# Attention block: the second key tile's mask taken out of the score matmuls and put behind the exponentials, three heads on GpSimd, one on VectorE

## The chip, the cores and the metric

One core of a Trainium2 chip runs the whole program. The metric is the device time in microseconds (us) of one execution. The engines work side by side, each through its own list of instructions in order: TensorE (PE) multiplies matrices into PSUM, ScalarE (ACT) does exponentials and copies, VectorE (DVE) and GpSimd (POOL) do elementwise work, SyncE (SP) issues the transfers.

## The reference, cut to what matters

A decoder block for 8 batches of 512 tokens with 256 features: a two-direction Mamba block, then attention with 16 heads, then a feed-forward block whose neurons spike over 5 steps. The parts around the change:

```python
scores = jnp.einsum('bhqd,bhkd->bhqk', q, k) / math.sqrt(D_HEAD)      # D_HEAD = 16
scores = jnp.where(mask == 0, jnp.float32(-1000000000.0), scores)
attn = jax.nn.softmax(scores, axis=-1)
out = jnp.einsum('bhqk,bhkd->bhqd', attn, v)
...
h = jnp.square(jax.nn.relu(jnp.einsum('bsd,fd->bsf', x, W_fc)))
y = jnp.einsum('bsf,df->bsd', h, W_proj)
def step(mem, _):                                   # 5 times, spikes are counted
    reset = spike_fn(mem - THRESHOLD)
    mem_new = BETA * mem + y - reset * THRESHOLD
    return (mem_new, spike_fn(mem_new - THRESHOLD))
```

## The kernel before, in words

The program has two passes. `mamba_pass` takes the first 1,600 us and isn't touched. `attention_pass` then loops over the 8 batches (`b`), about 135.6 us each. There is no scheduler: every engine's order is the order of the code, and semaphores (`wait_ge`, `then_inc`) tie them together.

A batch begins with 16 heads of prescores, of which DVE takes row maxima (L1897); between them PE does feed-forward work of the next batch. Then comes the **attention stage**, on which all of this document turns. It has 8 **units** (0 to 7); a unit is four heads (`hh` 0 to 3) and two key tiles of 128 keys (`t` 0 and 1), and it is done in two **halves** of two heads. PE's order in it is: `score(unit + 1, half)`, `weigh(unit, half)`, for both halves of all units, with a transpose (`to_tokens`, L1513) after the second `weigh` of units 2, 4 and 6.

- `score` (L1473) writes the two key tiles of a head into one of two PSUM pairs. A tile costs one matmul for the scores (`pair<-q_st,k_st`), and where it is masked there, a second that adds the mask (`pair<-mask_biasT,ident_bf`). A head waits until ACT has read the head before the last from its pair (`s_exp`).
- ACT (L1692) turns a pair into exponentials in `pr`, one instruction of 1024 columns a head.
- GpSimd (`mask_exp`, L2017, its instruction on L2024) multiplies the second tile of heads 1 and 3 by words that are 0 or 1. So those tiles have no mask matmul: `ON_POOL = ((1,), (3,))`, one head a half, from unit 1 on.
- `weigh` (L1490) multiplies `pr` by the values. Its first half takes the first key tile and waits for the unit's last exponential; its second half takes the second tile and waits for GpSimd's second mask of the unit (`s_kept`).

Meanwhile DVE counts the spikes of the batch before, on 128x1024 tiles: `start` (L1815), and four `step`s of three instructions each (L1825, L1827, L1829; step 1 has L1821 and L1823 instead of the first two), `finish` (L1834), which makes the output tile `tmp` that SP stores. Between them stand `norm_apply` (L1746), which writes `xn_q` for the next batch, and `normalise(g)` (L1799 and L1803), which waits for the transpose of unit 2g+2 (the last for the one after unit 7). GpSimd's part of the norm is `rstd_of` (L1972, L1974), ahead of its masks. After the stage, ACT's `project_k` (L1653) writes `qk`, which lies over `mem`, `cnt` and `tmp`; it waits for the store (`s_out`). The last batch has no next one, so no `norm_apply` and no `project_k`.

Of the kernel before, what the change touches and what calls it, by code (L numbers as in the profile page):

```python
# [14 lines left out]
H, DH = 16, 16  # L15
P = 128
# [6 lines left out]
QR = 6 * DH + 3  # L23
EPS = 1e-5
MASKED = -float(2 ** 32)
FLOOR = -3.0e38
STEPS, BETA, THRESHOLD = 5, 0.9, 1.0
# [13 lines left out]
_cols()  # L41


ON_POOL = ((1,), (3,))
Q_PART = [0, 0, 1, 0, 2, 1]
K_PART = [0, 1, 0, 2, 0, 1]

# [1118 lines left out]
def attention_pass(nc, ctx, a, mid, out, sb, where, stage, psum, consts, handover, early, late):  # L1166

    f32, bf16, i32 = mybir.dt.float32, mybir.dt.bfloat16, mybir.dt.int32
    ALU, ACT, AX = mybir.AluOpType, mybir.ActivationFunctionType, mybir.AxisListType
    ident, cols, minus_half, col, settle, s_const = consts  # L1170
    pair, bank, y_bank, general = psum
# [6 lines left out]
    pr = sb("pr", [P, 4, TT, T], f32, where["g1"])  # L1178
# [5 lines left out]
    y_sb = sb("y_sb", [P, TT, D])  # L1184
# [6 lines left out]
    mask_biasT = sb("mask_biasT", [P, TT, T], bf16)  # L1191
# [5 lines left out]
    q_st = sb("q_st", [P, H, T], bf16)  # L1197
    k_st = sb("k_st", [P, H, T], bf16)
# [12 lines left out]
    mem, cnt, tmp = (sb(name, [P, TT, D], f32, where["qk"] + 4 * KB * n)  # L1211
                     for n, name in enumerate(("mem", "cnt", "tmp")))
# [48 lines left out]
    m_cut = stage("m_cut", ahead=1)  # L1261
    s_sc = stage("score")
    s_exp = stage("exp", ahead=2)
    s_kept = stage("masked_exp")
    s_word = stage("mask_words")
    g_out = stage("g_out")
    out_ready = stage("out_ready")
# [1 line left out]
    with nc.Block() as block:  # L1269
# [102 lines left out]
        def _(pe):  # L1372
            pe.wait_ge(handover.sem, handover.count(0))

            def mm(o, lhsT, rhs, start=True, stop=True):
                return pe.matmul(o, lhsT, rhs, start=start, stop=stop)  # L1376
# [96 lines left out]
            def score(b, unit, half):  # L1473

                g, s = unit // 2, unit % 2
                if unit == H // 4 and half == 0:
                    pe.wait_ge(s_mr[1].sem, s_mr[1].count(b))
                for hh in (2 * half, 2 * half + 1):
                    hd = 4 * g + hh
                    n = b * 2 * H + unit * 4 + hh  # L1480
                    pe.wait_ge(s_exp.sem, s_exp.count(n - 2))
                    for t in range(2):
                        kt = 2 * s + t
                        on_pool = unit > 0 and t == 1 and hh in ON_POOL[half]
                        last = mm(pair[hh % 2][:, t, :], k_st[0:QR, hd, kt * P:(kt + 1) * P], q_st[0:QR, hd, :], True, on_pool)
                        if not on_pool:
                            last = mm(pair[hh % 2][:, t, :], ident_bf[:, :], mask_biasT[:, kt, :], False, True)
                    last.then_inc(s_sc.sem, 1)

            def weigh(b, unit, half, it):  # L1490

                g, s = unit // 2, unit % 2
                if half == 0 or unit == 0:
                    pe.wait_ge(s_exp.sem, s_exp.count(b * 2 * H + unit * 4 + 3))
                else:
                    pe.wait_ge(s_kept.sem, s_kept.count(b * (H - 2) + unit * 2 - 1))
                key = ("av", g)
                if s == 0 and half == 0:
                    pe.wait_ge(*G.free(key, it))
                bk = G.bank(key, it)  # L1500
                kt = 2 * s + half
                for hh in range(4):
                    last = mm(bk[32 * hh:32 * hh + 32, :], v_sb[:, kt, 4 * g + hh, :], pr[:, hh, kt, :],
                              kt == 0, kt == TT - 1)
                if kt == TT - 1:
                    last.then_inc(G.full_sem(key), 1)
# [45 lines left out]
            for k in range(TT):  # L1552
                last = mm(bank[0], ones_bf[:, :], keep_bf[:, k, :], k == 0, k == TT - 1)
# [167 lines left out]
        def _(dve):  # L1721
# [71 lines left out]
            def normalise(g, it):  # L1793

                dve.drain()
                dve.wait_ge(*G.full(("ot", g), it))
                bk = G.bank(("ot", g), it)
                o = bk[:, :].rearrange("p (j h e) -> p j h e", j=TT, h=4)
                dve.reciprocal(rsum[:, :, :], o[:, :, :, DH:DH + 1].squeeze(3))  # L1799
                dve.drain()  # L1800
                dst = o_sb[:, :, g * 4 * DH:(g + 1) * 4 * DH].rearrange("p j (h e) -> p j h e", h=4)
                for j in range(TT):
                    last = dve.tensor_tensor(dst[:, j], o[:, j, :, 0:DH],  # L1803
                                             rsum[:, j, :].unsqueeze(2).broadcast_to((P, 4, DH)), ALU.mult)
                last.then_inc(G.done_sem(("ot", g)), 1)

            def spikes(beta, cols_of=(A3,)):


                def start():  # L1810
                    dve.wait_ge(s_out.sem, s_out.count(beta - 1))
                    settle(dve)
                    dve.drain()
                    for c in cols_of:
                        dve.tensor_scalar(cnt[c], y_sb[c], THRESHOLD, None, ALU.is_gt)  # L1815

                def step(i):
                    for c in cols_of:
                        dve.drain()
                        if i == 1:  # L1820
                            dve.scalar_tensor_tensor(tmp[c], y_sb[c], BETA, y_sb[c], ALU.mult, ALU.add)  # L1821
                            dve.drain()
                            dve.scalar_tensor_tensor(mem[c], y_sb[c], THRESHOLD, tmp[c], ALU.is_gt, ALU.subtract)  # L1823
                        else:
                            dve.scalar_tensor_tensor(tmp[c], mem[c], -BETA, y_sb[c], ALU.mult, ALU.add)  # L1825
                            dve.drain()
                            dve.scalar_tensor_tensor(mem[c], mem[c], -THRESHOLD, tmp[c], ALU.is_lt, ALU.subtract)  # L1827
                        dve.drain()
                        dve.scalar_tensor_tensor(cnt[c], mem[c], -THRESHOLD, cnt[c], ALU.is_lt, ALU.add)  # L1829

                def finish():
                    dve.drain()
                    for c in cols_of:
                        dve.scalar_tensor_tensor(tmp[c], cnt[c], 1.0 / STEPS, x_res[c], ALU.mult, ALU.add).then_inc(out_ready.sem, 1)  # L1834
                return start, step, finish
# [52 lines left out]
            dve.memset(y_sb[A3], 0.0)  # L1888
            dve.memset(x_res[A3], 0.0)

            def batch(b, it, more):
                for hd in range(H):
                    for j in range(TT):
                        dve.wait_ge(s_max.sem, s_max.count((b * H + hd) * TT + j - 2))
                        dve.wait_ge(s_pre.sem, s_pre.count((b * H + hd) * TT + j))
                        settle(dve)
                        dve.tensor_tensor_reduce(  # L1897
                            masked[:, j % 2, :], bank[j], mask_bias[:, j, :], 1.0, FLOOR, ALU.add, ALU.max, m_col[:, j, hd:hd + 1]).then_inc(s_max.sem, 1)
                start, step, finish = spikes(b)
                if more:  # L1900
                    add_down(b + 1, it)
                    norm_stats(ATT, x1n)
                start()
                step(1)
                if more:
                    norm_apply(ATT, b + 1, x1n, xn_q)
                step(2)
                if isinstance(it, int):
                    dve.wait_ge(early.mid.sem, early.mid.count(B))
                normalise(0, it)  # L1910
                step(3)
                normalise(1, it)
                step(4)
                finish()
                normalise(2, it)
                normalise(3, it)
                if more:
                    cut_lo(b + 1, 0)

                dve.wait_ge(x1_set.sem, x1_set.count(b))  # L1920
                for jj in range(TT // 2):
                    dve.wait_ge(*G.full(("wo", jj), it))
                    bk = G.bank(("wo", jj), it)
                    dve.tensor_tensor(two(x_res, jj), two(x1, jj), bank_tiles(bk), ALU.add).then_inc(G.done_sem(("wo", jj)), 1)
                    dve.drain()
                    for j in (2 * jj, 2 * jj + 1):
                        dve.bn_stats(stats[:, j, :], x_res[:, j, :])
                norm_mean(FF2)
                if more:
                    cut_last(b + 1, 0)  # L1930
                    take_v(0, it)
                norm_apply(FF2, b, x_res, xn)
                if more:
                    take_q(it)
                    cut_lo(b + 1, 1)
                    take_v(1, it)
                    cut_last(b + 1, 1)
                    dve.wait_ge(*G.done(("fn", KD - 1), it))
                    first_norm(b + 2)
# [239 lines left out]
```

## Time and profile before

| what | value |
|---|---|
| median of 3 runs | 2750.9 us (2750.63 to 2751.59) |
| the profiled execution: its own time | 2753.34 us |
| its span, first to last instruction | 2751.6 us |
| mean granted TensorE clock | 0.982 |
| PE busy | 2629.1 us, 96% |
| DVE busy | 2192.3 us, 80% |
| ACT busy | 1742.5 us, 63% |
| POOL busy | 1719.2 us, 62% |

Busy shares are means over both passes. Rows of the timeline give start and duration in us; where one row holds several instructions (x4), its duration is from the first start to the last end. A time in brackets is how long the engine sat idle before the row, and for what. In the text "us 1982" means 1982 us after the span's start; batch 2 is the one that is read, and its attention stage runs from us 1967 to us 2012.

### The profile page before, as it was taken

How to read it: one execution, taken by the hardware profiler on the slowest of the kernel's cores; microseconds unless marked ns; L12 is line 12 of the kernel's file. 1: busy time of each engine (PE TensorE's matmuls, PEld its weight loads, DVE VectorE, ACT ScalarE, POOL GpSimd, SP SyncE). 2: the span in 40 equal slices, each digit the busy share in tenths (PEclk: the TensorE clock that was granted, in tenths of full speed). 3: DMA queues.
4: the chain of work that ended last, by engine and by line, in shares of the span. 5: the costliest groups of instructions: out<-in, count | busy, mean ns of one | idle time of the engine just before them, and what ended most of it. 6: DMA issues, size and time to landing. Idle time of an engine off the chain costs nothing. (4 is left out here: it accounts for less than half of the span.)

```text
span 2751.6 us, 55526 instructions
## 1 busy us (share of the span) xinstructions
PE 2629.1 (96%) x19177; PEld 1799.8 (65%) x19210; DVE 2192.3 (80%) x3270; ACT 1742.5 (63%) x2871; POOL 1719.2 (62%) x966
## 2 busy tenths in 40 slices
PE   6999999999999999999999879999999999999996
PEld 3887787787878877877887754545454545454523
DVE  5999999999999999999998949494848485858573
ACT  4878877877987788788778433545454444444342
POOL 3889989988988889899899813332323232323130
PEclk9999999999999999999999999999999999999978
DMA  3122212212221221222123051404040404040300
GB/s 123 43 79 73 85 44 81 89 43 79 74 80 43 80 82 58 70 67 95 37 78 102 9 182 55 123 2 122 2 122 2 122 2 122 2 122 2 107 2 16
DMA packets 102089, 187.07 MB, mean 68 GB/s; under 512 B 14720, under 2 KB 75264, under 8 KB 100256
## 3 DMA queue, kind: packets, MB, share of 16 engines
q1 hardware_dynamic: 101840, 183.92, 21.4%
q8 instruction: 135, 2.21, 0.3%
q14 instruction: 114, 0.93, 0.1%
HBM read 148.38 MB, written 35.52 MB: 67 GB/s over the span
## 5 line engine op out<-in xcount | busy, mean ns | idle before, releaser
L981 DVE TENSOR_TENSOR_SCAN h<-dA,pair 128x512 f32<-128x512 f32 x1024 | 1171.2, 1202 | 113.6 <-PE pair L475 102.9
L1120 POOL TENSOR_TENSOR hC<-h,C_rep 128x1024 f32<-128x1024 f32 x512 | 1201.4, 2368 | 93.5 <-DVE h L981 87.3
L718 ACT ACTIVATE dA<-delta,cols 128x511 f32<-128x511 f32 x1024 | 664.2, 711 | 41.7 <-DVE h L981 25.6
L475 PE MATMUL pair<-diagB,duT 64*128 64x128 f32 x8192 | 549.3, 281 | 23.1 <-DVE h L981 14.1
L475 PEld LDWEIGHTS pair<-diagB,duT 64*128 64x128 f32 x8192 | 485.9, 188 | 125.7 <-issue 90.1
L575 PE MATMUL y_bank<-ident,hC 128*128 128x128 f32 x4112 | 539.4, 278 | 5.0 <-POOL hC L1120 4.1
L575 PEld LDWEIGHTS y_bank<-ident,hC 128*128 128x128 f32 x4112 | 458.3, 141 | 96.9 <-issue 55.1
L1897 DVE CUSTOM_DVE_ANT_0 masked<-pair,mask_bias 128x512 f32<-128x512 f32 x512 | 321.8, 688 | 19.4 <-PE pair L1376 13.5
L1629 ACT ACTIVATE pr<-pair 128x1024 f32<-128x1024 f32 x256 | 248.3, 1021 | 74.3 <-PE pair L1376 74.3
L2001 POOL CAST m_part<-m_rest 8x512 bf16<-8x512 f32 x16 | 9.6, 603 | 414.4 <-ACT m_rest L1629 414.4
L475 PE MATMUL general<-xnT,w_in 128*128 128x512 f32 x496 | 241.9, 602 | 4.5 <-ACT xnT L718 3.5
L2024 POOL TENSOR_TENSOR pr<-pr,keep_word 128x512 int32<-128x512 int32 x112 | 162.7, 1455 | 117.6 <-ACT pr L1629 115.4
L1376 PE MATMUL general<-w_down,g 128*128 128x256 f32 x1024 | 232.5, 380 | 1.3 <-DVEq L1724 1.3
L1376 PEld LDWEIGHTS general<-w_down,g 128*128 128x128 f32 x1024 | 193.7, 190 | 33.8 <-issue 5.9
L1376 PE MATMUL pair<-q_st,k_st 99*128 99x512 bf16 x512 | 196.2, 383 | 5.5 <-ACT pr L1629 3.5
L1376 PE MATMUL general<-xT,w_up 128*128 128x512 f32 x360 | 168.2, 604 | 1.2 <-ACT xT L1629 0.7
L1376 PE MATMUL pair<-k_st,q_st 96*128 96x512 bf16 x512 | 151.6, 404 | 6.9 <-DMA q_st<-qk_parts 4.2
L991 DVE SCALAR_TENSOR_TENSOR u<-general,cols,u 128x511 f32<-128x511 f32 (+2 forms) x192 | 142.0, 740 | 13.3 <-ACT u L718 9.4
L1376 PE MATMUL pair<-mask_biasT,ident_bf 128*128 128x512 bf16 x368 | 140.3, 381 | 0.0
L1376 PEld LDWEIGHTS pair<-q_st,k_st 99*128 99x128 bf16 x512 | 50.1, 98 | 135.9 <-ACT pr L1629 91.0
L1972 POOL TENSOR_SCALAR rstd<-mv 128x4 f32<-128x4 f32 x24 | 15.6, 650 | 196.3 <-DVE mv L1739 193.7
L1376 PEld LDWEIGHTS pair<-k_st,q_st 96*128 96x128 bf16 x512 | 50.2, 98 | 113.2 <-DVE m_col L1897 83.5
(185 smaller groups left out, 3197.1 us busy)
## 6 DMA issues: line engine op xcount, KB each, us to landing
C_rep<-c_rows SPq DMA_DIRECT2D x128, 512.0 KB, 4.2
qk_parts<-qk_part SPq DMA_DIRECT2D x96, 256.0 KB, 4.2
w_in<-w_in SPq DMA_DIRECT2D x16, 1024.0 KB, 4.9
k_st<-qk_parts SPq DMA_DIRECT2D x8, 1536.0 KB, 9.1
q_st<-qk_parts SPq DMA_DIRECT2D x8, 1536.0 KB, 9.4
x_in<-x SPq DMA_DIRECT2D x18, 512.0 KB, 5.3
w_out<-w_out SPq DMA_DIRECT2D x17, 512.0 KB, 4.2
mid<-x_out SPq DMA_DIRECT2D x9, 512.0 KB, 4.8
```

The source lines that it names most:

```text
L475: return pe.matmul(o, lhsT, rhs, start=start, stop=stop)
L575: last = pe.matmul(y_bank[:, c * P:(c + 1) * P], hC[:, g % RING, i, c * P:(c + 1) * P], ident[:, :], start=j == 0 and i == 0 and c == 0, s ...
L718: return act.activation(o, i, fn, **kw)
L981: last = dve.tensor_tensor_scan(h[:, g % 4, i, :], dA[:, g % 4, i, :], dBu[:, i, :], 0.0, ALU.mult, ALU.add)
L991: dve.scalar_tensor_tensor(u[n][:, k, lag:T], raw[:, 0:T - lag], col("fb"[n] + "conv_w", CW * k + CW - 1 - lag), u[n][:, k, lag:T], ALU.mu ...
L1120: pool.tensor_tensor(hC[:, g % RING], h[:, g % 4], C_rep[:, 2 * j:2 * j + 2, :], ALU.mult).then_inc(s_hC.sem, 1)
L1376: return pe.matmul(o, lhsT, rhs, start=start, stop=stop)
L1629: return act.activation(o, i, fn, **kw)
L1897: dve.tensor_tensor_reduce(masked[:, j % 2, :], bank[j], mask_bias[:, j, :], 1.0, FLOOR, ALU.add, ALU.max, m_col[:, j, hd:hd + 1]).then_in ...
L1972: pool.tensor_scalar(rstd[:, :], mv[:, :, 1], EPS, None, ALU.add)
L2001: pool.tensor_copy(high, m_rest[:, :])
L2024: pool.tensor_tensor(words, words, keep_word[:, unit % 2, :].unsqueeze(1).broadcast_to((P, len(heads), T)), ALU.mult).then_inc(s_kept.sem, 1)
```

## The change

The second key tile of all four heads, from unit 1 on, is masked behind its exponential. GpSimd takes heads 0 and 1 in the first half (one instruction of two heads) and head 3 in the second. DVE takes head 2: a new `keep_exp(b, unit)` waits for that head's exponential and takes the minimum of it and mask plus 2^32 (2^32 where a key is kept, 0 where not). Its calls stand among the passes that count spikes; `step` now takes `parts`, so that calls can stand inside a step, and `finish` moves behind `normalise(2)` and `keep_exp(b, 7)`. `weigh` of a second half waits for both engines.

```diff
-ON_POOL = ((1,), (3,))
+ON_POOL = ((0, 1), (3,))
+ON_DVE = ((), (2,))
...
-                        on_pool = unit > 0 and t == 1 and hh in ON_POOL[half]
-                        last = mm(pair[hh % 2][:, t, :], k_st[0:QR, hd, kt * P:(kt + 1) * P], q_st[0:QR, hd, :], True, on_pool)
-                        if not on_pool:
+                        kept_later = unit > 0 and t == 1 and hh in ON_POOL[half] + ON_DVE[half]
+                        last = mm(pair[hh % 2][:, t, :], k_st[0:QR, hd, kt * P:(kt + 1) * P], q_st[0:QR, hd, :], True, kept_later)
+                        if not kept_later:
                             last = mm(pair[hh % 2][:, t, :], ident_bf[:, :], mask_biasT[:, kt, :], False, True)
...
                 else:
+                    pe.wait_ge(s_kept_dve.sem, s_kept_dve.count(b * (H // 2 - 1) + unit - 1))
                     pe.wait_ge(s_kept.sem, s_kept.count(b * (H - 2) + unit * 2 - 1))
...
+            def keep_exp(b, unit):
+
+                for half in range(2):
+                    for hh in ON_DVE[half]:
+                        dve.wait_ge(s_exp.sem, s_exp.count(b * 2 * H + unit * 4 + hh))
+                        exps = pr[:, hh, 2 * (unit % 2) + 1, :]
+                        dve.scalar_tensor_tensor(exps, mask_biasT[:, 2 * (unit % 2) + 1, :], -MASKED, exps,
+                                                 ALU.add, ALU.min).then_inc(s_kept_dve.sem, 1)
...
                 step(1)
+                keep_exp(b, 1)
                 if more:
                     norm_apply(ATT, b + 1, x1n, xn_q)
-                step(2)
+                step(2, (0, 1))
+                keep_exp(b, 2)
+                step(2, (2,))
+                step(3, (0,))
                 if isinstance(it, int):
                     dve.wait_ge(early.mid.sem, early.mid.count(B))
+                keep_exp(b, 3)
                 normalise(0, it)
-                step(3)
+                step(3, (1,))
+                keep_exp(b, 4)
+                step(3, (2,))
                 normalise(1, it)
-                step(4)
+                keep_exp(b, 5)
+                step(4, (0, 1))
+                keep_exp(b, 6)
+                step(4, (2,))
+                normalise(2, it)
+                keep_exp(b, 7)
                 finish()
-                normalise(2, it)
                 normalise(3, it)
```

DVE's order from the end of step 1, before (`pr` are the exponentials, `mem`, `cnt` and `tmp` the spikes' state, count and scratch; L1799 and L1803 are `normalise(0)`):

```order
L1829 SCALAR_TENSOR_TENSOR cnt<-mem,cnt 128x1024
L1746 TENSOR_SCALAR xn_q<-x1n,mv_7223,rstd_7224 128x256 [waits ln1_rstd]
L1746 TENSOR_SCALAR xn_q<-x1n,mv_7223,rstd_7224 128x256 x3
L1825 SCALAR_TENSOR_TENSOR tmp<-mem,y_sb 128x1024
L1827 SCALAR_TENSOR_TENSOR mem<-mem,tmp 128x1024
L1829 SCALAR_TENSOR_TENSOR cnt<-mem,cnt 128x1024
L1799 RECIPROCAL rsum<-general 128x16 [waits mid_dma,ot_full]
L1803 TENSOR_TENSOR x_out<-general,rsum 128x64 x4
```

The same place now (lines behind the new functions are 2 to 27 further down; L1904 is `keep_exp`):

```order
L1836 SCALAR_TENSOR_TENSOR cnt<-mem,cnt 128x1024
L1904 SCALAR_TENSOR_TENSOR pr<-mask_biasT,pr 128x512 [waits exp]
L1749 TENSOR_SCALAR xn_q<-x1n,mv_7223,rstd_7224 128x256 [waits ln1_rstd]
L1749 TENSOR_SCALAR xn_q<-x1n,mv_7223,rstd_7224 128x256 x3
L1827 SCALAR_TENSOR_TENSOR tmp<-mem,y_sb 128x1024
L1833 SCALAR_TENSOR_TENSOR mem<-mem,tmp 128x1024
L1904 SCALAR_TENSOR_TENSOR pr<-mask_biasT,pr 128x512 [waits exp]
L1836 SCALAR_TENSOR_TENSOR cnt<-mem,cnt 128x1024
L1827 SCALAR_TENSOR_TENSOR tmp<-mem,y_sb 128x1024
L1904 SCALAR_TENSOR_TENSOR pr<-mask_biasT,pr 128x512 [waits exp,mid_dma]
L1802 RECIPROCAL rsum<-general 128x16 [waits ot_full]
L1806 TENSOR_TENSOR x_out<-general,rsum 128x64 x4
```

The `keep_exp` of unit 1 now stands ahead of `xn_q`, and that of unit 2 behind `xn_q` and two of step 2's passes.

At the end of the stage DVE now has (the last pass of step 4, `normalise(2)`, unit 7, `finish`):

```order
L1836 SCALAR_TENSOR_TENSOR cnt<-mem,cnt 128x1024
L1802 RECIPROCAL rsum<-general 128x16 [waits ot_full]
L1806 TENSOR_TENSOR x_out<-general,rsum 128x64 x4
L1904 SCALAR_TENSOR_TENSOR pr<-mask_biasT,pr 128x512 [waits exp]
L1841 SCALAR_TENSOR_TENSOR tmp<-cnt,x_res 128x1024
```

Unit 7's instruction stands behind `normalise(2)`, which waits for the transpose after unit 6 (`ot_full`).

PE's second half of a unit, before (`score` of heads 2 and 3, then `weigh`):

```order
L1376 MATMUL pair<-q_st,k_st 128x512 [waits exp]
L1376 MATMUL pair<-mask_biasT,ident_bf 128x512
L1376 MATMUL pair<-q_st,k_st 128x512
L1376 MATMUL pair<-mask_biasT,ident_bf 128x512
L1481 REGISTER_ALU
L1376 MATMUL pair<-q_st,k_st 128x512 [waits exp]
L1376 MATMUL pair<-mask_biasT,ident_bf 128x512
L1376 MATMUL pair<-q_st,k_st 128x512
L1496 REGISTER_ALU
L1376 MATMUL general<-pr,v_sb 32x512 [waits masked_exp]
L1376 MATMUL general<-pr,v_sb 32x512 x3
```

And now:

```order
L1378 MATMUL pair<-q_st,k_st 128x512 [waits exp]
L1378 MATMUL pair<-mask_biasT,ident_bf 128x512
L1378 MATMUL pair<-q_st,k_st 128x512
L1483 REGISTER_ALU
L1378 MATMUL pair<-q_st,k_st 128x512 [waits exp]
L1378 MATMUL pair<-mask_biasT,ident_bf 128x512
L1378 MATMUL pair<-q_st,k_st 128x512
L1498 ISA
L1499 ISA [waits masked_exp_dve]
L1378 MATMUL general<-pr,v_sb 32x512 [waits masked_exp_pool]
L1378 MATMUL general<-pr,v_sb 32x512 x3
```

One mask matmul of the half is gone (six matmuls in `score` instead of seven; the first half likewise), and `weigh` has a second wait.

## Rows read from the trace of the kernel before

**Rows 1.** The page: busy times; the chain that ended last, by engine.

```profile
PE 2629.1 (96%) x19177; PEld 1799.8 (65%) x19210; DVE 2192.3 (80%) x3270; ACT 1742.5 (63%) x2871; POOL 1719.2 (62%) x966
...
PE 33%; DVE 3%; issue 2%; ACT 1%; POOLq 1%; DMA 1%; POOL 0%; DVEq 0%; ACTq 0%
```

**Rows 2.** The chain in order of time, us 1960 to 2100: start, duration, what.

```profile
1979.51 1.63 PE pair L1376 x7
...
2009.88 1.28 POOL pr L2024
2011.20 1.06 PE y_bank L1376 x8
```

**Rows 3.** Timeline of PE: start, duration, engine, line, operation, names, shapes.

```profile
1979.44 0.39 PE L1376 MATMUL pair<-q_st,k_st 99*128 99x512 bf16 x1
1979.67 0.38 PE L1376 MATMUL pair<-mask_biasT,ident_bf 128*128 128x512 bf16 x1
...
1982.07 0.39 PE L1376 MATMUL pair<-q_st,k_st 99*128 99x512 bf16 x1
...
1986.33 1.06 PE L1376 MATMUL y_bank<-pr,v_sb 128*32 128x512 f32 x8
```

**Rows 4.** Timeline of ACT: exponentials of units 1 and 2, then unit 3.

```profile
1975.27 1.94 ACT L1629 ACTIVATE pr<-pair 128x1024 f32<-128x1024 f32 x2 [0.73 <-PE pair L1376]
...
1982.35 0.60 ACT L1629 ACTIVATE xT<-general 128x512 f32<-128x512 f32 x1
1983.15 1.94 ACT L1629 ACTIVATE pr<-pair 128x1024 f32<-128x1024 f32 x2 [0.20 <-PE pair L1376]
```

**Rows 5.** Timeline of DVE: step 2 of the spikes, in batch 2.

```profile
1979.93 1.23 DVE L1825 SCALAR_TENSOR_TENSOR tmp<-mem,y_sb 128x1024 f32<-128x1024 f32 x1
1981.23 2.15 DVE L1827 SCALAR_TENSOR_TENSOR mem<-mem,tmp 128x1024 f32<-128x1024 f32 x1
1983.46 2.15 DVE L1829 SCALAR_TENSOR_TENSOR cnt<-mem,cnt 128x1024 f32<-128x1024 f32 x1
```

**Rows 6.** Timeline of POOL: the norm's `rstd`, then masks.

```profile
1974.54 1.96 POOL L1974 TENSOR_TENSOR rstd<-rstd,minus_half 128x4 f32<-128x4 f32 x1
...
1980.01 2.29 POOL L2024 TENSOR_TENSOR pr<-pr,keep_word 128x512 int32<-128x512 int32 x1 [0.64 <-ACT pr L1629]
1982.64 1.89 POOL L2024 TENSOR_TENSOR pr<-pr,keep_word 128x512 int32<-128x512 int32 x1 [0.34 <-ACT pr L1629]
```

**Rows 7.** Queries by line: durations in ns, min/median/max, first and last start.

```profile
L2024 POOL TENSOR_TENSOR pr<-pr,keep_word x112: 1262/1292/2302, 1705.7 to 2685.0; 128x512 int32<-128x512 int32 x112
...
L1984 POOL TENSOR_TENSOR x1n<-x_in,x_mid x8: 2350/2358/2365, 1607.8 to 2447.6; 128x1024 f32<-128x1024 f32 x8
...
L1746 DVE TENSOR_SCALAR xn_q<-x1n,mv,rstd x32: 401/414/1373, 1621.0 to 2521.7; 128x256 f32<-128x256 f32 x32
```

**Rows 8.** Timeline of DVE: a 512-column pass in the tail, GpSimd idle.

```profile
2731.09 0.69 DVE L1827 SCALAR_TENSOR_TENSOR mem<-mem,tmp 128x512 f32<-128x512 f32 x1
```

**Rows 9.** Timeline of DVE at the end of batch 2's stage: `normalise(2)`.

```profile
2009.99 0.26 DVE L1799 RECIPROCAL rsum<-general 128x16 f32<-128x16 f32 x1 [3.00 <-PE general L1513]
2010.33 0.62 DVE L1803 TENSOR_TENSOR x_out<-general,rsum 128x64 f32<-128x64 f32 x4
```

**Rows 10.** Timeline of PE: an idle stretch of the last batch.

```profile
2700.43 1.12 PE L1384 MATMUL general<-ident,xn 128*128 128x128 f32 x4 [5.10 <-DVE xn L1746]
```

**Rows 11.** Windows of 1 us there: length, PE, PEld, DVE, ACT, POOL busy, PEclk.

```profile
2698.00:2699.00 1.00, 0.00 (x0) 0.00 (x0) 0.01 (x1) 0.00 (x0) 0.96 (x1) 0.67 0.00 0
...
2707.00:2708.00 1.00, 1.00 (x2) 0.34 (x1) 0.00 (x0) 0.97 (x2) 0.00 (x0) 0.50 0.00 0
...
2709.00:2710.00 1.00, 1.00 (x4) 0.47 (x3) 0.00 (x0) 0.41 (x1) 0.00 (x0) 1.00 0.00 0
```

**Rows 12.** After the stage: ACT's `project_k`; the transfers' time to landing (median us).

```profile
2014.22 0.69 ACT L1629 ACTIVATE qk<-general,cols 128x512 f32<-128x512 f32 x1 [1.29 <-PE general L1376]
...
out<-tmp SPq DMA_DIRECT2D x8, 512.0 KB, 2.9
```

More of the change, by code:

```diff
@@ L1263, in attention_pass @@
     s_exp = stage("exp", ahead=2)
-    s_kept = stage("masked_exp")
+    s_kept = stage("masked_exp_pool")
+    s_kept_dve = stage("masked_exp_dve")
     s_word = stage("mask_words")
@@ L1815, in start, with step @@
                         dve.tensor_scalar(cnt[c], y_sb[c], THRESHOLD, None, ALU.is_gt)
-                def step(i):
+                def step(i, parts=(0, 1, 2)):
                     for c in cols_of:
-                        dve.drain()
-                        if i == 1:
-                            dve.scalar_tensor_tensor(tmp[c], y_sb[c], BETA, y_sb[c], ALU.mult, ALU.add)
+                        if 0 in parts:
                             dve.drain()
-                            dve.scalar_tensor_tensor(mem[c], y_sb[c], THRESHOLD, tmp[c], ALU.is_gt, ALU.subtract)
-                        else:
-                            dve.scalar_tensor_tensor(tmp[c], mem[c], -BETA, y_sb[c], ALU.mult, ALU.add)
-                            dve.drain()
-                            dve.scalar_tensor_tensor(mem[c], mem[c], -THRESHOLD, tmp[c], ALU.is_lt, ALU.subtract)
-                        dve.drain()
-                        dve.scalar_tensor_tensor(cnt[c], mem[c], -THRESHOLD, cnt[c], ALU.is_lt, ALU.add)
+                            if i == 1:
+                                dve.scalar_tensor_tensor(tmp[c], y_sb[c], BETA, y_sb[c], ALU.mult, ALU.add)
+                            else:
+                                dve.scalar_tensor_tensor(tmp[c], mem[c], -BETA, y_sb[c], ALU.mult, ALU.add)
+                        if 1 in parts:
+                            dve.drain()
+                            if i == 1:
+                                dve.scalar_tensor_tensor(mem[c], y_sb[c], THRESHOLD, tmp[c], ALU.is_gt, ALU.subtract)
+                            else:
+                                dve.scalar_tensor_tensor(mem[c], mem[c], -THRESHOLD, tmp[c], ALU.is_lt, ALU.subtract)
+                        if 2 in parts:
+                            dve.drain()
+                            dve.scalar_tensor_tensor(cnt[c], mem[c], -THRESHOLD, cnt[c], ALU.is_lt, ALU.add)
                 def finish():
```

## The prediction, made before the change was run

> **What bounds the kernel now.** The page first: PE is busy 96% of the span, and of the chain that ended last it has 33% of the span against 8% for everything else together [rows 1]. The chain in order of time shows what that means in the attention stage: PE's stretches follow each other without a wait, seven `score` matmuls in 1.63 us; only at the stage's end it goes through GpSimd, whose mask of unit 7 ends at us 2011.16 and frees the last `weigh` at 2011.20 [rows 2]. The timeline gives the pitch. `score` of a second half starts at 1979.44, the next half's at 1982.07: 2.63 us a half, of which a matmul takes 0.22 to 0.23 and 1.0 is `weigh` [rows 2, 3]. ACT has 0.7 us to spare in a half, but only 0.20 after the copy L1629 of every second unit [rows 4].
>
> **What the change takes from PE.** Two mask matmuls a unit. A half falls from seven matmuls to six, 2.63 to 2.41. That leaves ACT's copy (0.60) and two exponentials (1.83 to the copy's start) just enough room: 2.43 against 2.41 [rows 4]. Of 14 halves with unit 1 or later one is written while PE waits for exponentials of unit 0 anyway, so 13 count: 13 x 0.22 = 2.8 us a batch, 23 us in 8 batches, if nothing else becomes late.
>
> **What it adds, and where.** GpSimd's two heads in one instruction: its 128x1024 addition takes 2.36 us, one head 1.28 [rows 7]. A unit then costs it 3.64 of 4.82 us. DVE's 128x512 instruction with two SBUF inputs takes 0.69 [rows 8]. Each alone would fit. They don't stay alone. The spike passes take 1.23 or 2.15 us [rows 5], and set beside GpSimd's rows the two engines' long times explain each other. At 1979.93 DVE starts, GpSimd at 1980.01; DVE ends at 1981.16, GpSimd at 1982.30, 1.14 later. DVE's next, started at 1981.23, ends 1.08 after that, at 1983.38; GpSimd's mask of 1982.64 ends 1.15 after that, at 1984.53; DVE's of 1983.46 ends at 1985.61, again 1.08 after it [rows 5, 6]. So of a two-input DVE instruction and a GpSimd instruction only one runs, whole, and the other starts when it ends; the one that has waited longer comes next. `xn_q`'s four scalings obey this too: 0.41 us alone, up to 1.37 behind a mask [rows 7]. I call this the turn. The Trainium skill says the same (SBUF — State Buffer, Who interferes with whom): the port pair that DVE and GpSimd share is an exclusive lock for a whole instruction, taken also by a DVE instruction with two SBUF inputs. By that rule the change adds work to the one resource that both need; by counting each engine's load alone it would cost nothing, and the sum would be -23 us. The trace agrees with the rule.
>
> All that the change adds wants the turn. Durations after a wait: 1024-column pass 1.08, `keep_exp` 0.57 (0.69 less some 0.12, a little under what the 1.23 pass loses), one head 1.15, two heads 2.24 (likewise from 2.36), a scaling 0.15 (1.37 less a mask).
>
> **Walk to the first stall**, batch 2, times less 1900. ACT's unit 1 second half starts 0.22 earlier, at 75.05, so head 2's exponential is there at 76.1 [rows 4]. GpSimd's `rstd` ends at 76.50 [rows 6]. Then the turn goes: `keep_exp` 1 to 77.1; GpSimd unit 1 first half 79.3; scaling 79.5; GpSimd second half 80.6; scaling 80.8; unit 2 first half 83.0; scaling 83.2; second half 84.3; scaling 84.5; step 2's first pass, the turn being free, 84.56 to 85.8; unit 3 first half (its exponentials are there at 84.2, as PE isn't held yet) 88.0; step 2's second pass 89.1; unit 3 second half 90.3; `keep_exp` 2 to 90.8. PE wants that for the second `weigh` of unit 2. It has issued its last `score` by 85.5 (81.8 + 2.41 for unit 3's first half, then 1.3; a 0.3 us wait for GpSimd in unit 1 is in it), so it **stands still for 5.4 us**, from 85.5 to 90.9. Before, that `weigh` came at 86.33 [rows 3]: 4.6 late. Behind the wait stand unit 4's scores, which ACT needs, then GpSimd.
>
> **From there to the stage's end.** Unit 4's first exponentials reach GpSimd at about 95.5 (90.9 + `weigh` 1.0, transpose 0.5, three matmuls and latency 0.9, two exponentials 1.94, 0.17). From there the turn is the bound: GpSimd 4 x (2.24 + 1.15) = 13.6, DVE's four passes left 4.3, `keep_exp` 4 to 6 1.7, and some 1 us in which nobody asks: the last mask ends at 116.1. DVE's last pass of step 4 ends at 114.9; `normalise(2)` takes 0.96 [rows 9]; `keep_exp` 7 ends at 116.7, and the last `weigh` is at 116.8, against 111.2 before [rows 2]. The same walk with the code of before puts it at 111.4, so I count +5.4 a batch.
>
> **The clock.** A 5.4 us stall isn't only itself. PE stood idle for 5.10 us until 2700.43 [rows 10]; its granted clock was 0.67 in the window from 2698 and still 0.50, that is 1.2 GHz, at 2707, and full again at 2709 [rows 11]. Here PE resumes at 90.9 with work in one piece. At the low level 4 to 5.5 us of it do half: 2.0 to 2.7 us later, of which the chain of unit 4's scores hands on 1.5 to 2.4, since DVE catches up meanwhile. I take +1.9. The Trainium skill (TensorE: Matmul & The Clock Gate, Part 1) also has the array at 1.2 GHz after idling; that agrees.
>
> **After the stage.** `finish` now ends about 1.2 us after the last `weigh` starts, the store is issued 0.3 later and lands after 2.9 [rows 12]: 4.4 after `weigh`. ACT's first `project_k` was 3.0 after it (2014.22 against 2011.20) [rows 2, 12]. It starts 1.4 later; PE needs that bank only 5.4 after `weigh`, about when its copy ends. Nothing, then, and up to 1.6 a batch if the store lands 2 us later.
>
> **The sum.** Seven batches at 5.4 + 1.9 = 7.3 give 51; the last, without scalings, stalls only at unit 7 and comes out 1.6 late by the same walk. 53 us on the profiled execution's 2753.3 (span 2751.6) is 2806; its own time stands 2.4 above the median, so against the median 2750.9 + 53 = **2804 us**, slower by 1.9%. PE's saving is inside these figures, as the walk runs at the pitch of 2.41.
>
> **Rivals.**
> *The stall comes but the clock holds* (20%). For it: at 2695.3 to 2698 the clock held for most of 3 us of idling [rows 10, 11]. Against it: the stall is as long as the one that lowered it. 7 x 5.4 + 1.6 = 39: 2790.
> *The clock falls twice* (10%): PE also waits 2 us before the last `weigh`, in front of ACT's and PE's unhidden work there; with late stores up to 2.3 a batch more: 2820.
> *The turn costs about half of what I walk* (12%), if `keep_exp` 2 slips in one GpSimd instruction (2.2 us) sooner and the stall stays under 3 us: 5.4 - 2.8 = 2.6 a batch, 2770.
> *Faster* (7%): `keep_exp` doesn't wait for its turn and the masks don't delay DVE, so that every unit's second tile is ready in time. Only the tail's `normalise(2)`, then `keep_exp` 7, would show. -2.8 plus 0.4 a batch: 2732. It decides from `keep_exp` 2 ending before 85.6; I have it at 90.8, and rows 5 and 6 say it waits.
> *No change* (2%): a stall of 2.8 that pays back the saving.
> The forecast has 49%.
>
> **Range and chances.** 39 to 69 us for the cases with a full stall, and half a stall's 2770 is left to the tail below: 2778 to 2822 holds 80%. All but the last two rivals are slower. Slower by over 0.2% (5.5 us, about what a measurement of this kernel can tell): 0.91; within 0.2%: 0.02; faster: 0.07.
>
> **What would show it.** In the changed profile: `score` halves at a pitch of 2.41 where PE doesn't wait; PE idle for some 5 us ahead of a `weigh` near the stage's first third, released by DVE's `pr`; L1904 at up to 2 us and more, though 0.69 alone; GpSimd's two-head masks at 2.4 to 3.3; granted clock at 0.5 behind the stall; attention stages some 7 us longer and the last one 1 to 2. I am wrong if L1904 stays at 0.7 beside running masks, or if `xn_q`'s four scalings are over before unit 2's masks begin.

## The result, and the profile after

The changed kernel takes 2809.9 us (median of 4 runs, 2807.9 to 2810.4), the kernel before 2750.8; the ratio is 1.0212, 95% interval 1.02 to 1.0225. It is slower by 59 us; 53 were forecast.

The page of the changed kernel, its busy times and the chain by engine, as in [rows 1]:

```profile
PE 2632.0 (94%) x19065; PEld 1796.7 (64%) x19098; DVE 2302.2 (82%) x3326; ACT 1743.2 (62%) x2871; POOL 1797.7 (64%) x966
...
PE 28%; DVE 8%; DVEq 3%; issue 2%; ACT 1%; POOLq 1%; DMA 1%
```

DVE, with its queue, has gone from 3% to 11% of the span on the chain. Busy shares hardly moved. Now the same stretch of batch 2 as in [rows 5, 6], on DVE's timeline (this stage's first exponential starts at us 1981.59; before it was 1968.28, so these times are 13.3 later than those of the walk):

```profile
1989.41 0.69 DVE L1904 SCALAR_TENSOR_TENSOR pr<-mask_biasT,pr 128x512 f32<-128x512 bf16 x1 [0.51 <-ACT pr L1632]
1990.02 6.43 DVE L1749 TENSOR_SCALAR xn_q<-x1n,mv,rstd 128x256 f32<-128x256 f32 x4
1996.55 2.13 DVE L1827 SCALAR_TENSOR_TENSOR tmp<-mem,y_sb 128x1024 f32<-128x1024 f32 x1
1998.76 3.21 DVE L1833 SCALAR_TENSOR_TENSOR mem<-mem,tmp 128x1024 f32<-128x1024 f32 x1
2001.89 1.74 DVE L1904 SCALAR_TENSOR_TENSOR pr<-mask_biasT,pr 128x512 f32<-128x512 bf16 x1
2003.72 1.23 DVE L1836 SCALAR_TENSOR_TENSOR cnt<-mem,cnt 128x1024 f32<-128x1024 f32 x1
```

and on GpSimd's (four masks, then two):

```profile
1990.12 7.48 POOL L2051 TENSOR_TENSOR pr<-pr,keep_word 128x1024 int32<-128x1024 int32 x4 [0.32 <-issue]
1997.96 5.12 POOL L2051 TENSOR_TENSOR pr<-pr,keep_word 128x1024 int32<-128x1024 int32 x2 [0.36 <-ACT pr L1632]
```

The four scalings take 6.43 us for 0.41 each; unit 2's `keep_exp` ends at 2003.63, for 90.8 + 13.3 = 2004.1 in the walk. PE and the clock behind it, timeline and windows of 2 us (counts in brackets left out, the seventh number behind the window is the granted clock, 1.00 for 2.4 GHz and 0.50 for 1.2):

```profile
2003.76 1.82 PE L1378 MATMUL y_bank<-pr,v_sb 128*32 128x512 f32 x8 [4.89 <-DVE pr L1904]
...
2030.43 1.18 PE L1378 MATMUL y_bank<-pr,v_sb 128*32 128x512 f32 x8 [2.17 <-DVE pr L1904]
2031.54 3.52 PE L1378 MATMUL general<-ctxT,w_att 128*128 128x512 f32 x4
```

```profile
2004.00:2006.00 2.00, 2.00 (x11) 0.49 (x4) 1.93 (x2) 0.00 (x0) 0.00 (x0) 0.50 0.00 0
2006.00:2008.00 2.00, 2.00 (x9) 1.00 (x8) 1.73 (x7) 0.27 (x1) 0.00 (x0) 0.66 0.00 0
...
2031.00:2033.00 2.00, 2.00 (x10) 0.84 (x3) 0.61 (x1) 0.60 (x1) 0.00 (x0) 0.56 0.06 22
2033.00:2035.00 2.00, 2.00 (x4) 0.67 (x3) 0.00 (x0) 0.00 (x0) 0.00 (x0) 0.59 0.70 241
```

PE waits 4.89 us for unit 2's and 2.17 us for unit 7's tile. Both times the clock falls to 0.5: behind the first the eight matmuls of `weigh` take 1.82 us for 1.07, behind the second `project_k`'s four take 3.52 for 1.98.

Where the 56 us between the profiled spans (2807.7, 2751.6) are, from the starts of each batch's first exponential:

| stretch | before | after | difference |
|---|---|---|---|
| first pass, to batch 0 | 1697.1 | 1695.6 | -1.5 |
| batch 0 | 135.6 | 142.8 | +7.2 |
| batches 1 to 5 | 5 x 135.6 | 5 x 143.3 | +38.6 |
| batch 6 | 132.4 | 140.2 | +7.7 |
| batch 7, to its last instruction | 108.6 | 112.7 | +4.1 |

Batch 2 has +7.65: its last `weigh` starts 48.84 us after its first exponential, for 42.92, so the stage is 5.92 longer; 1.7 come after it.

### The profile page after: what moved, and what is told of

Its sections match the earlier page's. It is cut to its first block and busy times, and to the rows that moved or that the text cites. A ratio compares the mean times of both kernels' runs of the same rounds, so it can differ in the third digit from the quotient of the medians.

```text
span 2807.7 us, 55457 instructions
## 1 busy us (share of the span) xinstructions
PE 2632.0 (94%) x19065; PEld 1796.7 (64%) x19098; DVE 2302.2 (82%) x3326; ACT 1743.2 (62%) x2871; POOL 1797.7 (64%) x966
## 5 line engine op out<-in xcount | busy, mean ns | idle before, releaser
L2051 POOL TENSOR_TENSOR pr<-pr,keep_word 128x1024 int32<-128x1024 int32 x112 | 242.0, 2178 | 80.7 <-ACT pr L1632 77.7
L1378 PE MATMUL pair<-q_st,k_st 99*128 99x512 bf16 x512 | 183.1, 391 | 6.2 <-ACT pr L1632 3.4
L992 DVE SCALAR_TENSOR_TENSOR u<-general,cols,u 128x511 f32<-128x511 f32 (+2 forms) x192 | 142.0, 740 | 13.3 <-ACT u L719 9.3
L1972 DVE COPY y_sb<-general 128x512 f32<-128x512 f32 x16 | 11.1, 692 | 141.3 <-PE general L1378 141.3
L1378 PE MATMUL y_bank<-pr,v_sb 128*32 128x512 f32 x512 | 76.1, 668 | 53.9 <-DVE pr L1904 53.9
```

The lines of the kernel that those rows point to most:

```text
L992: dve.scalar_tensor_tensor(u[n][:, k, lag:T], raw[:, 0:T - lag], col("fb"[n] + "conv_w", CW * k + CW - 1 - lag), u[n][:, k, lag:T], ALU.mu ...
L2051: pool.tensor_tensor(words, words, keep_word[:, unit % 2, :].unsqueeze(1).broadcast_to((P, len(heads), T)), ALU.mult).then_inc(s_kept.sem, 1)
```

## The experiments

Each kernel is the changed one, edited as shown. Its ratio is to the kernel before, timed beside it (median 2751.4 us beside e1 to e4, 2753.3 beside e5 to e8). `e4`, `e5` and the like stand for the full names.

**e1_fill: is the low clock a cost of its own?**

```diff
                 else:
+                    if not isinstance(it, str) and unit in (2, 7):
+                        other = ("ot", {2: 0, 7: 3}[unit])
+                        pe.wait_ge(*G.free(other, it))
+                        for _ in range({2: 20, 7: 8}[unit]):
+                            mm(G.bank(other, it)[:, :], ident_bf[:, :], mask_biasT[:, 0, :])
                     pe.wait_ge(s_kept_dve.sem, s_kept_dve.count(b * (H // 2 - 1) + unit - 1))
```

> Only the clock is changed: while PE waits for VectorE, it runs matmuls whose result nobody reads, 20 ahead of unit 2's second weigh (20 x 0.22 = 4.4 us of the 4.9 us stall) and 8 ahead of unit 7's (1.8 of 2.2 us), in the first seven batches. If the low clock behind the two stalls costs what I think, the granted clock stays at 1.00 there, project_k's four matmuls take 1.98 us again and not 3.52, and a batch is 1.4 to 1.7 us shorter at the first stall and 1.5 at the second: some 20 us in all, 2786 to 2793. If the low clock costs nothing because VectorE and GpSimd bound the stage anyway, only the second one counts: about 2799. If the stalls alone are the cost, no change: 2810.

Measured: 2794.0 us (2786.8 to 2795.2), ratio 1.0148 (1.0131 to 1.0165): 16 us less than the changed kernel. Its timeline of PE and a window behind each stall (here that of 2001 and of 2026):

```profile
2000.20 1.07 PE L1378 MATMUL y_bank<-pr,v_sb 128*32 128x512 f32 x8 [0.59 <-DVE pr L1909]
...
2025.88 1.06 PE L1378 MATMUL y_bank<-pr,v_sb 128*32 128x512 f32 x8 [0.52 <-DVE pr L1909]
2026.88 1.98 PE L1378 MATMUL general<-ctxT,w_att 128*128 128x512 f32 x4
```

```profile
2001.00:2003.00 2.00, 2.00 (x14) 0.97 (x10) 1.93 (x3) 0.46 (x1) 0.00 (x0) 1.00 0.00 0
...
2026.00:2028.00 2.00, 2.00 (x11) 0.68 (x9) 1.07 (x1) 0.60 (x1) 0.00 (x0) 1.00 0.00 0
```

DVE's tiles come as late as before, but the clock holds, and `weigh` and `project_k` are fast again. A batch from 1 to 5 takes 140.6 us for 143.3. The stage is 4.96 us longer than before the change, for 5.92: the first fall costs 0.96, not the 1.4 to 1.7 expected. A faster PE meets DVE's lateness sooner: it waits 0.39 us at unit 6, where it had not waited, and is held 2.36 us for 2.17 at unit 7, filling counted. The second costs 1.65, as it stands where PE is the bound. The total came out just above the upper end for two reasons. The last batch, which has no fill, lost 2.8 us more than in the changed kernel. And batch 0 gained 0.3 us instead of 2.7: there the clock held too, but the store of `out` landed 6.2 us after the last `weigh` began, for 4.4 in the other batches, and `project_k`, which waits for it, came late enough to hold PE for 1.47 us:

```profile
1749.26 0.69 ACT L1637 ACTIVATE qk<-general,cols 128x512 f32<-128x512 f32 x1 [4.58 <-DMA out<-tmp]
```

**e2_gpsimd_part and e3_vector_part: one half of the change alone.** In the first, `ON_DVE` is empty and DVE's order that of before; in the second:

```diff
-ON_POOL = ((0, 1), (3,))
+ON_POOL = ((1,), (3,))
```

> GpSimd's part alone: heads 0, 1 and 3 on GpSimd, head 2 again with its mask matmul, VectorE's order as before. PE has 7 matmuls less a batch, 1.5 us. Turns (a two-input VectorE instruction and a GpSimd one exclude each other): the two-head masks and the spike passes delay each other, GpSimd ends unit 7 about 2.3 us late, and the saving is used up: +0.7 us in each of seven batches, -0.5 in the last, 2751 to 2760. Rival, each engine's load alone: -12 us, 2739.

> VectorE's part alone: head 2 by keep_exp in the order of the change, GpSimd has heads 1 and 3 as before, head 0 has its mask matmul. Turns: seven keep_exp of 0.57 us and one-head masks fit, no stall but 0.9 us at unit 7: -0.95 us a batch, 2743 (2740 to 2750). Rival, that VectorE's waits for exponentials and its new order are what makes it late whatever GpSimd does: the stall at unit 2 stays, 2780 or more.

Measured: GpSimd's part 2758.5 us (2756.0 to 2760.9), ratio 1.0028 (1.0018 to 1.0039), slower; VectorE's part 2744.5 (2742.9 to 2748.6), 0.9978 (0.9968 to 0.9987), faster. PE's timeline at the end of batch 2's stage in e2_gpsimd_part, and the durations of `keep_exp` in e3_vector_part (ns, min/median/max):

```profile
2014.58 1.06 PE L1378 MATMUL y_bank<-pr,v_sb 128*32 128x512 f32 x8 [2.36 <-POOL pr L2039]
```

```profile
L1904 DVE SCALAR_TENSOR_TENSOR pr<-mask_biasT,pr x56: 677/679/1079, 1702.3 to 2676.2; 128x512 f32<-128x512 bf16 x56
```

Alone, either half nearly fits. With GpSimd's two-head masks its last mask ends 2.36 us after PE asks for it, as worked out; some 3 of the 7.7 us are the clock, which fell behind this wait in batches 0 and 3. VectorE's `keep_exp` waits at most 0.4 us. Slower by 7.7 and faster by 6.0 us don't add to slower by 59: the loss is in the two together.

**e4_no_gpsimd_masks and e5_no_spike_passes: take away what either engine does in the turn.** For the first:

```diff
-                words = pr[:, heads[0]:heads[-1] + 1, kt, :].bitcast(i32)
+                words = pr[:, heads[0]:heads[-1] + 1, kt, 0:8].bitcast(i32)
```

with eight columns of `keep_word` to match, so that most of those tiles stays unmasked; for the second:

```diff
                 keep_exp(b, 1)
...
-                step(2, (0, 1))
                 keep_exp(b, 2)
-                step(2, (2,))
-                step(3, (0,))
...
                 keep_exp(b, 3)
                 normalise(0, it)
-                step(3, (1,))
                 keep_exp(b, 4)
```

and so on for the rest of steps 3 and 4: nine spike passes are left out of the stage.

> The changed kernel, but GpSimd's masks cover 8 of 512 columns, so the rest of heads 0, 1 and 3 in those tiles stays unmasked; order, waits and semaphores are the same. Turns: VectorE never waits for long, keep_exp of unit 2 is in time, no stall there, half pitch 2.41 us, only 0.8 us at unit 7: -2.4 us a batch, 2732 (2728 to 2738). Rival, VectorE's own order is late by itself: a stall at unit 2 of over 2 us stays and the time is over 2765.

> The changed kernel without the nine spike passes of steps 2 to 4 inside the attention stage (spikes are counted over two steps there); keep_exp, xn_q and GpSimd's two-head masks are all in. Turns: what is left (23.7 us of masks, 4.0 of keep_exp, 0.6 of scalings, 1.1 of finish) fits in the stage, no stall at unit 2, 1.0 us at unit 7: -2.0 us a batch, 2735 (2730 to 2742). Rival, that two-head masks or keep_exp's waits alone make the stall: over 2765.

Measured: e4 2734.4 us (2732.4 to 2737.0), ratio 0.9941 (0.9925 to 0.9958); e5 2736.2 us (2734.9 to 2739.3), ratio 0.994 (0.9923 to 0.9957). `keep_exp` of e4, then of e5:

```profile
L1904 DVE SCALAR_TENSOR_TENSOR pr<-mask_biasT,pr x56: 679/691/694, 1701.9 to 2663.5; 128x512 f32<-128x512 bf16 x56
```

```profile
L1904 DVE SCALAR_TENSOR_TENSOR pr<-mask_biasT,pr x56: 691/1565/1772, 1701.4 to 2666.8; 128x512 f32<-128x512 bf16 x56
```

In e4 DVE does all that it does in the changed kernel, in the same order, and none of its 56 `keep_exp` takes over 0.70 us, for a longest of 2.83 in the changed kernel. PE waits for it at unit 7 alone, 0.72 us. So DVE's own load and order aren't the cause of the loss. In e5 GpSimd does all its masks and half of the `keep_exp` take over 1.5 us, but DVE has little else: PE waits 0.88 us at unit 7. In both the stage is shorter than before the change, by 2.4 us in e4 (40.53 for 42.92) and 2.0 in e5 (40.96): PE's 2.8 less most of the wait at unit 7.

**e6_mask_matmuls_too: what is PE's saving worth here?**

```diff
-                        kept_later = unit > 0 and t == 1 and hh in ON_POOL[half] + ON_DVE[half]
+                        kept_later = unit > 0 and t == 1 and hh in ((1,), (3,))[half]
```

> The changed kernel with the two mask matmuls of a unit put back on PE, GpSimd and VectorE masking the same tiles again: what the change adds without what it takes. Turns: the stage ends with the last turn, so PE's 23 us are worth nearly nothing; the stall at unit 2 is 2.6 us instead of 4.9, and the clock falls behind it all the same: 2800 to 2818, the changed kernel's 2810 within 8. Rival, PE's work adds up: 2810 + 23 = 2833.

Measured: 2813.1 us (2809.9 to 2814.6), ratio 1.0212 (1.0195 to 1.0229), the changed kernel's ratio to the last digit. The stall wasn't the 2.6 us that I expected. PE waits 4.34 us at unit 2 and 1.64 at unit 7:

```profile
2007.30 1.19 PE L1378 MATMUL y_bank<-pr,v_sb 128*32 128x512 f32 x8 [4.34 <-DVE pr L1904]
```

```profile
2035.18 1.07 PE L1378 MATMUL y_bank<-pr,v_sb 128*32 128x512 f32 x8 [1.64 <-DVE pr L1904]
2036.18 1.98 PE L1378 MATMUL general<-ctxT,w_att 128*128 128x512 f32 x4
```

The stage of batch 2 is 1.5 us longer (50.3 for 48.8), those of the other batches from 1 to 6 by 1.4 to 2.0, so PE's 2.8 us a batch are worth half to two thirds of themselves in it. Most of that comes back behind it: after 1.64 us of waiting the clock doesn't fall, in any of the seven batches, and `project_k` takes 1.98 us.

**e8_unit2_early: is one place in DVE's order the fault?**

```diff
-                step(2, (0, 1))
                 keep_exp(b, 2)
-                step(2, (2,))
-                step(3, (0,))
+                step(2)
...
                 keep_exp(b, 3)
+                step(3, (0,))
                 normalise(0, it)
```

> The changed kernel with unit 2's keep_exp straight behind xn_q, so that it isn't late, and step 3's first pass behind unit 3's. Turns: the work that wants a turn is the same, so the stall moves to unit 3 with 5 us: 2800 to 2815, no gain. Rival, that the place of unit 2's keep_exp is the fault: the 4.9 us stall and its slow clock go, 2751 + 7 x 2 = 2765 or less.

Measured: 2813.0 us (2812.1 to 2814.0), ratio 1.0215 (1.0198 to 1.0232). Unit 2 is in time, and PE waits 4.6 us for unit 3 instead:

```profile
2008.65 1.94 PE L1378 MATMUL y_bank<-pr,v_sb 128*32 128x512 f32 x8 [4.59 <-DVE pr L1904]
```

The stall moves; it doesn't go. This is one other order; that no order would do is not shown.

**e7_vector_part_unit7_first: a version that beats both kernels.** As e3_vector_part, and:

```diff
-                normalise(2, it)
                 keep_exp(b, 7)
+                normalise(2, it)
                 finish()
```

> VectorE's part alone as in e3_vector_part, with unit 7's keep_exp ahead of normalise(2). The 0.9 us wait ahead of the last weigh goes: -1.5 us a batch, 8 batches, 2739 (2735 to 2743), faster than both kernels. If something else holds the last weigh: 2744, as e3_vector_part.

Measured: 2742.9 us (2738.0 to 2743.7), ratio 0.9956 (0.9942 to 0.997). A batch takes 134.1 us, for 134.7 in e3_vector_part and 135.6 before; the 0.88 us wait ahead of the last `weigh` is gone but for 0.26, for GpSimd:

```profile
2008.26 1.06 PE L1378 MATMUL y_bank<-pr,v_sb 128*32 128x512 f32 x8 [0.26 <-POOL pr L2051]
```

It is 12 us faster than the kernel before in the ratio. Over e3_vector_part it gains 4 us by the batches; the medians lie 1.6 apart, and this difference isn't settled by them: the two were timed on different chips, and the untouched first pass alone differs by 4 us between the two profiled executions.

## Why the prediction was right

**The turn.** Right, and shown: taking either side's work out of it (e4, e5) removes the whole loss, halving the change (e2, e3) removes nearly all, and the one reordering tried (e8) only moves it. The walk put unit 2's late `weigh` at 90.9; it came at 90.45 (2003.76 less 13.3). It had one detail wrong: the first `keep_exp` didn't wait for `rstd` (0.69 us at 1989.41), so that one scaling slipped in ahead of the first mask and the rest came 0.45 us sooner.

**The walk's +5.4 a batch.** 4.96 with the clock held (e1_fill).

**The clock in the stage, +1.9.** Measured 0.96 in batch 2, half of it. I had taken "4 to 5.5 us" of work at the low level without a row for it; in batch 2 the clock was full again 3.6 us after PE restarted (0.82 in the window from us 2007 to 2008, so low for 0.36 of it), and of the 1.8 us that PE lost in them DVE's lateness hid nearly half.

**After the stage, nothing.** This step failed. I had a second fall of the clock as a rival at 10%, with "up to 2.3 a batch"; it happened behind six of the seven stages (not behind batch 0's, where it was the stage itself that took 1.2 us more) and cost 1.65. The late store, which I looked at instead, was indeed hidden. It landed 4.4 us after the last `weigh` began, as worked out; in those six batches the slow PE was later still, and in batch 0, as in six batches of e1_fill, ACT waited for the store but PE did not wait for ACT. The price that I had named for a store 2 us later, up to 1.6, is what batch 0 of e1_fill paid (1.7).

**The last batch, +1.6.** It was +4.1. My walk had it stall only at unit 7, and this was wrong: PE waited 2.48 us for unit 3 as well, and the clock fell even behind that; I had let it fall only behind stalls of about 5 us.

Batches of 4.96 + 0.96 + 1.65 = 7.6 for my 7.3, and 4.1 for 1.6. That the clock's two terms nearly cancel (1.9 + 0 forecast, 0.96 + 1.65 measured) is luck; the stall itself is not. Seven batches and the last together are 5 us over the forecast, the first pass gives 1.5 back, and the rest of the six us between forecast and result is that the medians lie 59 us apart where the profiled spans lie 56. The rival of full gain (-19 us) would have needed that `keep_exp` doesn't wait; e4 comes nearest to that kernel, and it runs at 2734 for my 2732.

## What to carry to other kernels

Before moving work to an idle-looking VectorE or GpSimd, add up what both do with two SBUF inputs (and VectorE's fast scalings) as if it were one engine's work, instruction by instruction, since the one waits for the whole of the other's instruction. Longer instructions on one side make each wait on the other longer: step 2's second pass took 3.21 us beside two-head masks, 2.15 beside one-head ones. And price a stall of TensorE at its own length plus what the low clock costs after it, most of all where the next work is TensorE's own.

## What the runs showed of the hardware that I had not expected

- The clock fell behind waits of 2.17 and 2.48 us too, and in e8_unit2_early behind 2.05 to 2.10 us in all seven batches. It held behind one of 2.06 in batch 0 of the changed kernel and behind the 1.6 us ahead of the last `weigh` in e6_mask_matmuls_too's batches 0 to 6. In e2_gpsimd_part one and the same wait of 2.3 to 2.4 us was followed by a fall in batches 0 and 3, which took 1.6 and 1.4 us longer, and by none in the other five:

```profile
2016.00:2018.00 2.00, 2.00 (x9) 1.13 (x8) 0.00 (x0) 0.71 (x2) 0.00 (x0) 1.00 0.09 28
...
2152.00:2154.00 2.00, 2.00 (x7) 0.70 (x3) 0.00 (x0) 0.60 (x1) 0.00 (x0) 0.52 0.26 89
```

The first window is just behind that wait in batch 2, the second in batch 3. So at waits of 2.0 to 2.5 us either can happen.
- Behind the 4.34 us stall of e6_mask_matmuls_too `weigh` still ran nearly at full clock (1.19 us) and the fall came after it (granted clock 1.00 in the window to 2008, 0.53 in the next 2 us): it can follow a stall that is already over. In e8_unit2_early it came before the end: 0.50 in the window from 2007, when PE restarted at 2008.65.
- `rstd`'s tiny instruction, listed with 1.96 us, doesn't hold VectorE up to its listed end: in all seven batches `keep_exp`, which started 0.4 us before that end, took 0.69 us. It is the one place seen where the turn as I put it doesn't hold; why stays open.
